# Ranks and own places made ahead of the heads, first loads in order of use, and 79 expert tiles in place of 80

## The reference, cut to what matters

```python
x = layernorm(x + attn(x))
x = layernorm(x + mlstm(x, ctx, ctx))   # C = (q k^T) * D, h = C v / normalizer
logits = flat @ router_w.T
_, topk_idx = top_k(logits + router_bias, 2)
out = sum_e combine[:, e] * (silu(flat @ Wu[e]) * (flat @ Wg[e])) @ Wd[e]
out = out + silu(flat @ Su) * (flat @ Sg) @ Sd
x = layernorm(x + out)
```

## Time and profile before

| what | value |
|---|---|
| median of 3 runs | 2054.07 us (2053.21 to 2058.03) |
| the profiled execution's own time | 2052.97 us |
| its span, first to last instruction | 2051.4 us |
| TensorE matmuls busy | 1860.1 us, 91% |
| VectorE, ScalarE, GpSimd busy | 1146.8, 646.0, 692.8 us |
| mean granted TensorE clock | 0.952 |
| DMA | 226.47 MB, mean 110 GB/s |

### The profile page before, as it was taken

How to read it: one execution, slowest core, us unless ns; L and a number is a source line. 1 busy time by engine, 2 the same in 40 slices (tenths; PEclk the granted TensorE clock), 3 DMA queues, 4 the chain that set the end, 5 groups by cost and what they waited for, 6 DMA issues and landing times. The chain is left out here.

```text
span 2051.4 us, 35492 instructions
## 1 busy us (share of the span) xinstructions
PE 1860.1 (91%) x11010; PEld 1192.4 (58%) x11011; DVE 1146.8 (56%) x2410; ACT 646.0 (31%) x1358; POOL 692.8 (34%) x754
## 2 busy tenths in 40 slices
PE   3879999999999999999999999998789999999990
PEld 2556575766657676665767667576455444444440
DVE  2467766676676667766766776775532222222225
ACT  0152333424233342433435243343302212221224
POOL 3124233242323324232242413233224444444440
PEclk8889999999999999999999999999889999999995
DMA  8254343443424334242443424234415676556449
GB/s 278 57 118 111 63 101 85 99 121 60 120 62 100 94 91 119 60 120 62 99 110 78 126 52 120 72 71 93 129 57 107 128 180 175 127 121 145 89 77 338
DMA packets 151788, 226.47 MB, mean 110 GB/s; under 512 B 32448, under 2 KB 107200, under 8 KB 149056
## 3 DMA queue, kind: packets, MB, share of 16 engines
q1 hardware_dynamic: 101616, 132.94, 24.8%
q0 software_dynamic: 38336, 92.38, 19.9%
q10 hardware_dynamic: 11792, 0.61, 0.4%
HBM read 94.70 MB, written 48.83 MB: 70 GB/s over the span
## 5 line engine op out<-in xcount | busy, mean ns | idle before, releaser
L1592 PE MATMUL ps<-ug_w,rowsT 128*128 x640 | 293.1, 601 | 7.9 <-SPq L1441 4.5
L481 POOL DMA_INDIRECT routed_ids<-pair_w,pos_w x64 | 64.0, 999 | 485.4 <-DVE pair_w L764 438.6
L1592 PEld LDWEIGHTS ps<-ug_w,rowsT 128*128 128x128 f32 x640 | 122.7, 193 | 164.1 <-issue 164.1
L1481 POOL DMA_INDIRECT sum_rows<-y_sb,pairs x80 | 127.3, 1591 | 248.6 <-DVE y_sb L1559 139.5
L1082 PE MATMUL ps<-wqkv_sb,xT_sb 128*128 128x256 f32 (+1 forms) x512 | 172.1, 490 | 15.9 <-ACT maskr_sb L529 15.9
L975 DVE SCALAR_TENSOR_TENSOR weighted<-ps,decay 128x384 f32<-128x384 f32 x256 | 140.4, 554 | 75.1 <-PE ps L1208 68.1
L886 DVE RECIPROCAL arden<-ps 128x256 f32<-128x256 f32 x64 | 112.5, 1758 | 114.5 <-PE ps L1336 104.9
L627 ACT ACTIVATE decay<-ps,g_col 128x256 f32<-128x256 f32 x256 | 121.6, 475 | 171.5 <-PE ps L1191 120.4
L1547 DVE SCALAR_TENSOR_TENSOR silu<-tanh,ps 128x256 f32<-128x256 f32 x80 | 33.7, 421 | 252.0 <-ACT tanh L1502 252.0
L868 DVE TENSOR_REDUCE smax<-ps 128x2 f32<-128x512 f32 x256 | 164.0, 682 | 15.6 <-PE ps L1265 15.6
L1265 PE MATMUL ps<-k_stack,q_stack 96*128 96x256 f32 x512 | 121.2, 349 | 43.7 <-DVE weighted L975 15.2
(11 more groups left out here) (253 smaller groups left out, 3673.4 us busy)
## 6 DMA issues: line engine op xcount, KB each, us to landing
q_stack<-qkT_hi SPq DMA_DIRECT2D x128, 128.0 KB, 3.9
mk_stack<-ctxT_hi SPq DMA_DIRECT2D x128, 128.0 KB
mq_stack<-qkT_hi SPq DMA_DIRECT2D x128, 128.0 KB, 2.4
ug_w<-in_expert_ug SPq DMA_DIRECT2D x16, 1024.0 KB, 5.8
xT_sb<-in_xT SPq DMA_DIRECT2D x16, 512.0 KB, 3.3
x_sb<-in_x POOLq DMA_DIRECT2D x16, 512.0 KB, 3.7
ctxT_sb<-in_ctxT POOLq DMA_DIRECT2D x16, 512.0 KB, 4.0
q_stack<-qkT_lo SPq DMA_DIRECT2D x64, 128.0 KB, 4.9
```

Of the source, the lines that this page charges most:

```text
L1481: pool.indirect_dma_start(out=sum_dram, out_offset=bass.IndirectOffsetOnAxis(ap=tables.pairs[:, m, 0:1], axis=0), in_=y_sb[:, m % W, :], i ...
L1592: ins = nc.tensor.matmul(ps[:, 2 + k % 2, :], rowsT[:, k % 2, c, :], ug_w[:, bass.ds(slot, 1), c, :].rearrange("p o n -> p (o n)"), start= ...
```

## The change

1. **Tiles.** The loops of the experts run over `TILES` = 79; the tables keep 80 columns. The rolled loop ends a round of four earlier, and the last three tiles are written out behind it.
2. **Ranks.** `rank` goes to bank 0, runs between `ug(1)` and `ug(2)`, and waits for `chosen` alone. `read_ranks` and `place_own` run ahead of `hidden(3)`, before head 0. `place_chosen` is cut in two: its first two operations run behind head 0, the other three (`place_gaps`) behind head 1, and `place_pairs` behind head 2. `qk2_mm(0)`, which writes bank 0, waits for `ranks_read`; the waits for it at `s_mm(1)` and `turn_den` go.
3. **Loads.** `xT_sb` and four pieces of `wqkv_sb` are issued first, with a semaphore for each piece; `qkv(0)` waits piece by piece. TensorE waits for the other 11 loads only before its first transposes. SyncE waits for these 11 to land before it issues `late`; GpSimd waits for the last piece of `wqkv_sb` before its first load.
4. **Gate weights.** `gw_hi` and `gw_lo` are made after the first turn; `gate_mm` waits for them (count 12).

```diff
-MT = (N * TOPK + E * (P - 1)) // P
-MT += -MT % 4
+TILES = (N * TOPK + E * (P - 1)) // P
+MT = TILES + -TILES % 4
...
-        RANKS_AT, PLACES_AT, GAP_AT, SHARES_AT = 1, 1, 7, 13
+        PLACES_AT, GAP_AT, SHARES_AT = 0, 7, 13
...
+            sp.dma_start(xT_sb[:, :, :], xT[0]).then_inc(xT_in.sem, 16)
+            for c in range(KC):
+                sp.dma_start(wqkv_sb[:, c, :], wqkv[:, c, :]).then_inc(wqkv_in[c].sem, 16)
             sp.wait_ge(consts.sem, 1)
-            sp.dma_start(xT_sb[:, :, :], xT[0]).then_inc(xT_in.sem, 16)
             for dst, src in first:
                 sp.dma_start(dst, src).then_inc(first_in.sem, 16)
+            sp.wait_ge(first_in.sem, 11 * 16)
             for dst, src in late:
...
+            pool.wait_ge(wqkv_in[KC - 1].sem, 16)
             pool.dma_start(x_sb[:, :, :], x_v[0]).then_inc(x_in.sem, 16)
...
-            run(act, body)
+            def split_gates():
+                act.wait_ge(gsum.sem, 8)
+                nc.scalar.copy(gw_hi[:, :, :], gw_f[:, :, :]).then_inc(gwhi.sem, 1)
+
+            run(act, body, split_gates)
...
+                    if w is not None and y is not None:
+                        read_ranks(ranks_of_turn)
+                        place_own()
                     if w is not None:
                         hidden(3)
...
-                            if w is not None and h == RANKS_AT:
-                                read_ranks(7)
                             if w is not None and h == PLACES_AT:
-                                place_own()
+                                place_chosen()
                             if w is not None and h == PLACES_AT + 1:
-                                place_chosen()
+                                place_gaps()
                             if w is not None and h == PLACES_AT + 2:
                                 place_pairs()
...
             whole(0, None, None)
+            dve.wait_ge(gwhi.sem, 1)
+            nc.vector.tensor_tensor(gw_lo[:, :, :], gw_f[:, :, :], gw_hi[:, :, :].bitcast(F32), ALU.subtract).then_inc(gwlo.sem, 1)
             whole(1, 0, None)
...
-            pe.wait_ge(first_in.sem, 12 * 16)
-            pe.wait_ge(consts.sem, 3)
...
+                            if t == 0 and lo == 0 and y is None:
+                                pe.wait_ge(wqkv_in[c].sem, 16)
...
-                def rank(bank):
+                def rank(out):
                     wait(pe, chosen_done, w, 1)
-                    if bank == 7:
-                        wait(pe, hT_done, w, SC)
...
                     for c in range(1, SC):
+                        if y is not None and c == 2:
+                            rank(ranks_of_turn)
                         ug(c)
...
                     if h == 0:
+                        if w is not None:
+                            wait(pe, ranks_read, w, 1)
...
-                        if w is not None and h == 0:
-                            rank(7)
...
-            with eng.Fori(2, MT // W) as r:
+            with eng.Fori(2, TILES // W) as r:
                 for j in range(W):
                     step(r * W + j, 2 * W + j)
-            for n in range(MT, MT + lags):
+            for n in range(TILES // W * W, TILES + lags):
                 step(n, n)
```

More of the change, by code:

```diff
@@ L251, in attention_and_mlstm @@
         ps = ctx.enter_context(nc.psum_tensor("ps", [P, 8, 512], F32))
-        first_in, late_in = sig("first_in", 12 * 16), sig("late_in", 7 * 16)
+        ranks_of_turn = ps[:, 0, 0:2 * ST * E]
+        first_in, late_in = sig("first_in", 11 * 16), sig("late_in", 7 * 16)
+        wqkv_in = [sig(f"wqkv_in{c}", 16) for c in range(KC)]
         consts = sig("consts", 1)
@@ L328, in qk2_bank, with run @@
             return 3 if h % 2 and not FIRST_S <= h < MAXIMA_AT else 0
-        def run(eng, body):
+        def run(eng, body, then=None):
             body(0, None, None, True)
+            if then is not None:
+                then()
             body(1, 0, None, True)
@@ L356, in _ @@
         def _(sp):
-            first = [(wqkv_sb[:, :, :], wqkv), (id_sb[:, :], ident), (cos_sb[:, :, :], rope_cos), (sin_sb[:, :, :, :], rope_sin),
+            first = [(id_sb[:, :], ident), (cos_sb[:, :, :], rope_cos), (sin_sb[:, :, :, :], rope_sin),
                      (mask_sb[:, :], mask), (gw_raw, gate_w), (iota_sb[:, :], iota), (before_sb[:, :], before),
@@ L526, in _ @@
         def _(act):
-            act.wait_ge(first_in.sem, 12 * 16)
+            act.wait_ge(first_in.sem, 11 * 16)
             nc.scalar.copy(idr_sb[:, :], id_sb[:, :]).then_inc(consts.sem, 1)
             nc.scalar.copy(maskr_sb[:, :], mask_sb[:, :]).then_inc(consts.sem, 1)
-            act.wait_ge(gsum.sem, 8)
-            nc.scalar.copy(gw_hi[:, :, :], gw_f[:, :, :]).then_inc(gwhi.sem, 1)
             act.wait_ge(pro.sem, 2 + GQ)
@@ L716, in over_e, with read_ranks @@
                     return v[:, :, :, :].rearrange("p k t e -> p (k t) e")
-                def read_ranks(bank):
+                def read_ranks(out):
                     wait(dve, ranks_ready, w, 1)
-                    nc.vector.tensor_copy(ranks[:, :, :, :], ps[:, bank, 0:2 * ST * E].rearrange("p (a t e) -> p a t e", a=2, e=E))\
+                    nc.vector.tensor_copy(ranks[:, :, :, :], out.rearrange("p (a t e) -> p a t e", a=2, e=E))\
                         .then_inc(ranks_read.sem, 1)
@@ L923, in front @@
                     if last:
-                        read_ranks(0)
+                        read_ranks(ps[:, 0, 0:2 * ST * E])
                         place_rows()
@@ L1114, in route @@
                     ins.then_inc(lg_ready.sem, 1)
[L1116 removed]
+                def rank(out):
                     wait(pe, chosen_done, w, 1)
[L1118 to L1119 removed]
                     flat = chosen[:, :, :].rearrange("p t e -> p (t e)")
[L1121 to L1122 removed]
+                    nc.tensor.matmul(out[:, 0:ST * E], before_sb[:, :], flat, start=True, stop=True)
+                    nc.tensor.matmul(out[:, ST * E:2 * ST * E], ones_k[:, 0:1].to_broadcast([P, P]), flat, start=True, stop=True)\
                         .then_inc(ranks_ready.sem, 1)
@@ L1244, in turn_den @@
                         wait(pe, m_lo_done, b, 1)
-                    elif w is not None:
-                        wait(pe, ranks_read, w, 1)
                     for t in range(ST):
@@ L1259, in s_mm @@
                         wait(pe, weighted_done, y, FIRST_S)
-                    if k == 1 and w is not None:
-                        wait(pe, ranks_read, w, 1)
                     if k >= 2:
@@ L1485, in _ @@
             pool.wait_ge(tables.ready, 1)
-            for m in range(MT + LAG):
-                if m < MT:
+            for m in range(TILES + LAG):
+                if m < TILES:
                     gather(m)
@@ L1532, in step @@
                     copy_rowsT(n, k)
-                if not isinstance(n, int) or W <= n < MT:
+                if not isinstance(n, int) or W <= n < 2 * W:
                     fetch(n + W, k + W)
@@ L1629, in _ @@
                 step(n, n, 16 * (n // W + 1))
-            with pe.Fori(2, MT // W) as r:
+            with pe.Fori(2, TILES // W) as r:
                 for j in range(W):
                     step(r * W + j, 2 * W + j, r * 16 + 16)
-            for n in range(MT, MT + 3):
-                step(n, n, None)
+            for n in range(TILES // W * W, TILES + 3):
+                step(n, n, 16 * (n // W + 1))
 def finish(nc, block, sum_dram, tables, out):
```

30 lines of the change are left out of this document (16 added, 14 removed).

## The result

The changed kernel takes 2019.97 us (median of 4 runs, 2018.02 to 2021.02) against 2055.70 of the kernel before on the same chip (4 runs, 2053.21 to 2058.03): ratio 0.9832, 95% interval 0.9814 to 0.9849, 31 to 38 us less. Predicted were 2014 us, 2005 to 2030, so the sum was 6 us too good. The profiled execution took 2020.32 us, its span is 2018.8; that of before was 2051.4, and the difference, 32.6 us, is what the traces have to account for.

The account below looks back on a forecast made before the run. TensorE was taken as the bound, so time comes only from its waits or low clock. 18.9 + 14 + 2 + 5.8 = 40.7 off 2052.97 gives 2012.3; with 1.1 for the median 2013.4, said as 2014, range 2005 to 2030.

Parts of the forecast that it names:

- Ranks, 16.2 for twelve turns: VectorE's rank and place work leaves the stretch before head 3: `s_mm`'s stall at head 4 goes, 1.35 us a turn.
- clock, 14: Behind head 4's stall: most low-clock stretches of the twelve turns stay away, 14 of 16.4 us; bounds 0 and 16.4.
- The cover on VectorE: Ahead of `hidden(3)`: 1.29 us of moved work fits 1.24 us of idle time, the excess lost in head 0's wait.
- the slower rival: Rival 4: TensorE waits for `chosen` before `ug(2)`, against 7.7 us in hand; 2073 at 11 us late; chance 0.03.
- the other bodies: The turn before the twelve and the last two bodies gain 0.9 us each from the moved ranks, 2.7 together.
- Tiles, 5.8: At the experts, one tile less takes 5.8 us off the path; bounds 5 and 6.
- Start, +2: Start: first matmul at about 6 or 7 us, `s_mm(0)` 2 us earlier; bounds 1 lost and 9.4 gained.
- the next thing to be late: At the start, the DMA, its engines fully busy from 2.10 to 32.40 us, limits the gain once the first matmul moves.
- The same bytes have to move: Start's DMA: unused 1.9 and 1.1 us close, less 1.5 for the new gap, so `s_mm(0)` moves by 1.5 us.
- Rival 3: Start gains in full if `late` does not hold the copies into `q_stack`: 7.4 us more, 2006; chance 0.08.
- the sum, 40.7: Whole kernel: ranks with the other bodies 18.9, clock 14, start 2 and tiles 5.8 us saved.

Follow-up runs that it names:

- the part alone: The kernel before with one part only: ranks and places, ratio 0.9849; tiles, 0.9966; first loads and the gate weights' split, 1.0008.
- the stall filled: The kernel before plus ten unread matmuls on TensorE ahead of its wait for `weighted` in each turn: 0.9911, 18.8 us less than before.
- brought back: The changed kernel plus one 176-column reciprocal on VectorE behind head 2's in each turn: ratio 0.9924 against the kernel before.
- `late` moved: The changed kernel with SyncE's `late` loads issued behind the first turn's twelve copies into `q_stack`: 2008.93 us, ratio 0.9781 against the kernel before.
- the one without SyncE's wait: The changed kernel without SyncE's wait for the first loads ahead of `late`: ratio 0.9836 against the kernel before.
- one small edit more: On top of `late` moved: GpSimd's four fills put behind its first-turn `k_stack` copies, 0.9825; or four `q_stack` copies issued by ScalarE, 0.9811.

## Why the prediction came out as it did

**Ranks, 16.2 for twelve turns, and clock, 14: right.** Together 30.2 predicted, 30.6 in the traces, 31.0 (26.5 to 35.5) by the part alone, which includes the other three bodies. A turn at clock 1.00 gained 87.93 - 86.63 = 1.30 where I took 1.35, and the low stretches fell from nine turns to one. The cover on VectorE held, and TensorE's wait for `chosen`, the slower rival, is not among the rows after. For the other bodies I had 2.7; they gave 0.0, 0.1 and 1.9. That the clock rose because the stall went was only argued in the prediction; the kernels with the stall filled and brought back now show it, on another chip.

**Tiles, 5.8: right.** 7.0 (4.1 to 9.7) by the part alone; between the two traces 4.2, since the experts of the changed kernel had two low stretches (at 1654.8 and 1822.0 us) where those of before had one.

**Start, +2: the wrong step.** Measured -3.7 between the two traces, -1.6 (+0.6 to -3.7) by the part alone. I had named the next thing to be late rightly, the copies behind `late`, and the gap of 2 us that the new waits open. The step that failed is "The same bytes have to move": I took them to keep the engines busy as long as before, and let 1.9 us and 1.1 us of unused time close, less 1.5 for the gap. The unused time did shrink, from 2.7 to 2.5 us with the new gap in it; but the same bytes took 44.4 us in place of 41.8. So `s_mm` comes 2.4 us later and not 1.5 sooner. The longer busy time is no accident of one trace: five kernels with the old order have 41.8 to 42.5 us, three with the new one 44.4 to 44.5. The trace of before left less unused than the other four of the old order (3.2 to 5.7 us), which is why on the mean `s_mm` is only 0.4 us later. About 1.0 us of it is `wqkv_sb`, which in four pieces moves in 512 packets of 3 KB (5.0 us of the engines) in place of 128 of 12 KB (3.9); 1.3 are the 8 KB packets of `late`, 11.25 us in place of 9.95 for the same 512; the rest is spread over the others. Behind `s_mm` comes one more stretch of low clock, 2.2 us, of which the next turn gives 0.8 back. The addition of 2.42 us on VectorE that had been 0.49 decided nothing: in the kernel with the new loads alone it is 0.49, the first copy is issued 3.0 us sooner, and `s_mm` comes 0.5 us sooner. I had also taken the copies to stand behind `late` already before; they were issued only when it had landed. Rival 3 put a number on a full gain, 9.4 us; it needed the reordering of `late`, which the change lacks: with it `s_mm` came 9.6 us sooner than before.

**The 8.1 us between the sum, 40.7, and the 32.6 of the two traces** are 5.7 at the start, 0.7 of the other bodies, 1.6 of the experts and 0.5 behind them, less 0.4 that the twelve turns gave on top. Nothing large was made good by luck: the one term that failed is most of the miss. By the ratio the gain is nearer 35, and the rest of the miss is chance between two executions.

## What to carry to other kernels

Read the granted clock by turns: a stall of 1.2 us on TensorE that recurs in every turn cost twice its own length here, and filling it with useless matmuls won 18.8 us, more than half of the 31.0 that removing it won (on another chip). When the first use is moved ahead, list what the same queue carries between it and the next thing that is late: work that starts sooner can land behind loads that used to be through. Moving seven loads behind twelve small copies won 10.5 us on top of the reordered first loads, which alone won nothing. Before timing by a row of a group, find out how many instructions one call leaves.

## What the runs showed of the hardware

- An addition of 128x320 elements on VectorE, with both operands in SBUF, takes 0.49 us alone and 2.42 us when it starts while GpSimd's 2.34 us subtraction runs (20.14 and 19.88 us, rows above). With `late` moved it met the last 0.8 us of it and took 1.12. In the eleven kernels in which this addition ran clear of it, it took 0.49. The Trainium skill, "GPSIMD Engine Reference", section "1. Specifications", says the two engines share their SBUF interfaces and collide where a VectorE instruction has two SBUF inputs; the rows agree.
- SyncE's issues of 128 KB copies take 0.69 us each, and 1.1 us each with 8 KB packets of earlier loads still in the queue (12 issues in 8.2 and 13.35 us).
- The kernel before takes 2053.66, 2111.41 and 2120.50 us on three chips, 3% more on two of them. All eight kernels traced on those two have ScalarE starting about 1.1 us late at one and the same instruction in 9 to 11 of the twelve turns, and none of the six traced on the first has. No other kernel was run on two chips, so whether a gain carries over is not shown: the changed kernel has 0.9832 on the first and the one without SyncE's wait 0.9836 on the second, but `late` moved has 0.9781 on the first, and with one small edit more 0.9825 on the second and 0.9811 on the third.
